# Half of an output projection taken into the attention loop, residual adds moved to GpSimd, eight output buffers

## The reference, cut to what matters

```python
xn = _layernorm(x, axis=-1)
q = _split_heads(xn @ q_w.T + q_b, 16) / sqrt(16)     # k and v the same, unscaled
attn = softmax(einsum('bhqd,bhkd->bhqk', q, k))
ctx = einsum('bhqk,bhkd->bhqd', attn, v)              # back to (1, 4096, 256)
attention = ctx @ out_w.T + out_b
acc = matmul(quant_fp8(xn), quant_fp8(weight).T)
ffn = bfloat16(acc * (x_scale * w_scale) + bias)
out = x + attention + ffn
```

## Time and profile before

| | us |
|---|---|
| three runs | 1885.83 (median), 1885.39, 1886.12 |
| the profiled execution | 1886.19 |
| its span | 1884.4 |
| ACT busy | 1764.0 (94%) |
| PE busy | 1647.7 (87%) |
| DVE busy | 1561.3 (83%) |
| POOL busy | 23.0 (1%) |

### The profile page before, as it was taken

One profiled execution on the slowest core, in us unless ns is written; L12 is line 12 of the kernel. 1 busy time (PEld: TensorE's weight loads), 2 busy tenths in 40 slices (PEclk: granted clock), 3 DMA queues, 4 the chain that ended last, 5 costly groups with the idle time before them and its releaser, 6 DMA issues.

```text
span 1884.4 us, 74586 instructions
## 1 busy us (share of the span) xinstructions
PE 1647.7 (87%) x33418; PEld 556.7 (30%) x33418; DVE 1561.3 (83%) x1924; ACT 1764.0 (94%) x1944; POOL 23.0 (1%) x41
## 2 busy tenths in 40 slices
PE   7988888888888888888888888888888888888888
PEld 4632222222222222222222222222222222222226
DVE  8687878978787888878787987878888887878788
ACT  2389999999999999999999999999999999999990
POOL 0000000000000000000000000000000000000000
PEclk9999999999999999999999999999999999999999
DMA  6430100000010000000010000001000000001003
GB/s 195 159 91 10 32 10 21 14 18 24 18 24 10 24 12 16 24 18 24 10 31 8 17 20 18 24 10 31 10 23 12 18 24 18 24 10 26 13 14 107
DMA packets 94965, 57.19 MB, mean 30 GB/s; under 512 B 55280, under 2 KB 87280, under 8 KB 94640
## 3 DMA queue, kind: packets, MB, share of 16 engines
q1 hardware_dynamic: 94160, 52.18, 10.3%
q10 hardware_dynamic: 480, 0.20, 0.0%
HBM read 30.54 MB, written 17.30 MB: 25 GB/s over the span
## 4 chain that ended last, share of the span: by engine, by line
ACT 52%; issue 33%; PE 12%; DVE 3%; ACTq 1%; DMA 0%; SPq 0%; DVEq 0%
ACT probs L667 52%; PE banks L1300 3%; PE banks L1259 3%; PE banks L1156 3%; PE banks L1388 1%; PE banks L1167 1%; ACTq L666 1%; DVE o_junk L951 1%; DVE o_sb L950 1%; PE banks L1378 0%; DVE xn_all L821 0%; DMA qk_bias<-in_L_attn_k_b_dram 0%; PE banks L1140 0%; DVE stats L736 0%; DVE x8T L834 0%
## 5 line engine op out<-in xcount | busy, mean ns | idle before, releaser
L667 ACT ACTIVATE probs<-banks 128x1024 f32<-128x1024 f32 x1888 | 1730.9, 1192 | 0.1
L1300 PE MATMUL banks<-probs,v_st 64*32 64x512 f32 x15104 | 1003.8, 590 | 2.2
L1259 PE MATMUL banks<-q_st,k_st 50*32 50x512 f16 x16384 | 792.4, 381 | 212.2 <-ACT probs L667 209.2
L1259 PEld LDWEIGHTS banks<-q_st,k_st 50*32 50x32 f16 x16384 | 232.6, 89 | 1145.5 <-ACT probs L667 1088.9
L984 DVE SCALAR_TENSOR_TENSOR horner<-horner,bits 128x1024 f32<-128x1024 f32 x320 | 393.0, 1228 | 11.0
L1300 PEld LDWEIGHTS banks<-probs,v_st 64*32 64x32 f32 x15104 | 272.0, 106 | 66.8 <-DVE o_junk L951 11.5
L971 DVE TENSOR_SCALAR bits<-banks 128x1024 int32<-128x1024 f32 x160 | 196.0, 1225 | 76.5 <-PE banks L1259 76.3
L984 DVE SCALAR_TENSOR_TENSOR horner<-bits 128x1024 f32<-128x1024 f32 x160 | 196.1, 1226 | 5.5
L989 DVE SCALAR_TENSOR_TENSOR d_probs<-horner,powers 128x1024 f32<-128x1024 f32 x160 | 196.0, 1225 | 5.5
L950 DVE COPY o_sb<-banks 128x512 f32<-128x512 f32 x32 | 22.2, 692 | 130.9 <-PE banks L1300 97.9
L980 DVE TENSOR_SCALAR bits<-bits 128x1024 int32<-128x1024 int32 x160 | 111.1, 694 | 5.5
(11 more groups left out here) (103 smaller groups left out, 428.1 us busy)
## 6 DMA issues: line engine op xcount, KB each, us to landing
k_st<-k_parts SPq DMA_DIRECT2D x102, 64.0 KB, 2.2
q_st<-q_parts SPq DMA_DIRECT2D x198, 32.0 KB, 1.9
k_st<-k_parts SPq DMA_DIRECT2D x102, 60.0 KB, 2.2
q_st<-neg_row SPq DMA_DIRECT2D x264, 1.0 KB, 1.7
xnT_copy<-probs SPq DMA_DIRECT2D x8, 512.0 KB, 3.1
q_parts<-x8T SPq DMA_DIRECT2D x16, 256.0 KB, 3.0
k_parts<-x8T SPq DMA_DIRECT2D x16, 256.0 KB, 2.4
w_f<-xnT_copy SPq DMA_DIRECT2D x16, 256.0 KB, 2.9
```

The costliest lines, as they stand in the source:

```text
L667: act.activation(probs[:, at:at + WIDE * CHUNK].rearrange("p (t c) -> p t c", t=WIDE), banks[:, bank:bank + WIDE, :], ACT.Exp, bias=EXP_SHIFT,
L1259: last = pe.matmul(banks[cols, bank + g, :], k_st[rows, keys], blocks[rows, j], start=True, stop=True, tile_position=(g * GROUP, t * VCOLS))
L1300: last = pe.matmul(banks[VCOLS * qb:VCOLS * (qb + 1), 6 + half, cols], v_st[keys, kt, :], src[keys, g * CHUNK:(g + 1) * CHUNK][:, cols], s ...
```

## The change

- A unit of the sampled pass has one more place, `OUT_AT` = 63, so 66 in all. In heads 0 to 7 PE does nothing there and DVE gives the buffer back with a semaphore increment. In heads 8 to 15 PE multiplies the finished half k = 0 of `ctxT` with its half of the output weights for two token tiles: two tiles x two row halves x four column quarters, 16 matmuls with 256 columns in f32 (32 instructions), of which eight work on different tiles of the array. The two row halves land in the two banks of the buffer. DVE adds both banks to the two rows of x in `x_all` with two adds, the second waiting for the first. 16 units times two tiles are all 32 token tiles.
- In DVE's order this stands behind the fifth block and ahead of the quantising and the take of the sums.
- Waits on the count of score places are counted without the new place (`scores_given`).
- In the output stage PE projects only the half k = 1. The add of x to the feed-forward term goes from DVE to GpSimd. DVE's L1087 waits for the group before to be added there.
- There are eight output buffers in place of two. They lie in `probs`.
- The second pass, which isn't run, loads x again.

```diff
+    OUT_AT = 63
+    OUT_BUFS = 4
-        o_out = [qt[0], qt[1]]
+        o_out = [probs[:, i * CHUNK:(i + 1) * CHUNK] for i in range(2 * OUT_BUFS)]
...
-                for p in range(PAIRS + (not full)):
+                for p in range(PAIRS + 2 * (not full)):
                     if p == MAX_AT and not full:
                         order.append(None)
+                    elif p == OUT_AT and not full:
+                        order.append(())
...
+            def outputs(again):                       # gpsimd
+                for i, g in enumerate(OUT_ORDER):
+                    n = again * GROUPS_OUT + i
+                    for b in range(2):
+                        t0 = g * CT + 2 * b
+                        pool.wait_ge(y_done, n * 2 + (b + 1 + 2))
+                        pool.wait_ge(out_ready, n * 2 + (b + 1))
+                        pool.tensor_tensor(res[b][:, :].rearrange("p (t d) -> p t d", t=2), x_all[:, t0:t0 + 2, :],
+                                           y_sb[b].rearrange("p (t d) -> p t d", t=2), ALU.add).then_inc(res_done, 1)
...
+                def output_part(h, u):                # vector
+                    n = u * c.places + OUT_AT
+                    if h < FROM_HEAD:
+                        dve.sem_inc(c.d_taken, 1)
+                        dve.wait_ge(c.d_taken, taken_at(h, u, OUT_AT))
+                        return
+                    bank, t0 = take_bank(h, n), part_tiles(h, u)
+                    rows = x_all[:, t0:t0 + 2, :].rearrange("p t d -> p (t d)")
+                    dve.wait_ge(part_done, t0 // 2 + 1)
+                    dve.tensor_tensor(rows, banks[:, bank, :], rows, ALU.add).then_inc(part_added, 1)
+                    dve.wait_ge(part_added, t0 // 2 + 1)
+                    dve.tensor_tensor(rows, banks[:, bank + 1, :], rows, ALU.add).then_inc(c.d_taken, 1)
+                    dve.wait_ge(c.d_taken, taken_at(h, u, OUT_AT))
...
+                        output_part(h, u)
                         if u:
                             quantise_part(h)
                         sums(h, u, lk + MAX_LINKS)
...
+                        dve.wait_ge(res_done, n * 2 + (b + 1))
...
-                    for b in range(2):
-                        t0 = g * CT + 2 * b
-                        dve.wait_ge(y_done, n * 2 + (b + 1 + 2))
-                        dve.tensor_tensor(res[b][:, :].rearrange("p (t d) -> p t d", t=2), x_all[:, t0:t0 + 2, :],
-                                          y_sb[b].rearrange("p (t d) -> p t d", t=2), ALU.add).then_inc(res_done, 1)
-                        dve.wait_ge(out_saved[b], n * 16 + OUT_0)
-                        dve.tensor_tensor(o_out[b][:, :], banks[:, 2 + b, :], res[b][:, :], ALU.add
+                        dve.wait_ge(out_saved[n % OUT_BUFS * 2 + b], n // OUT_BUFS * 16 + OUT_0)
+                        dve.tensor_tensor(o_out[n % OUT_BUFS * 2 + b], banks[:, 2 + b, :], res[b][:, :], ALU.add
                                           ).then_inc(out_ready, 1)
...
+                def output_part(h, n):                # tensor
+                    if h < FROM_HEAD:
+                        return
+                    u, bank, t0 = n // c.places, WIDE * ((h * c.head_places + n) % BUFS), part_tiles(h, n // c.places)
+                    buffer_free(h, n)
+                    pe.wait_ge(ctx_saved[t0 // CT % UNITS], SAVES * FROM_HEAD)
+                    for j in range(2):
+                        g, i = divmod(t0 + j, CT)
+                        t = g // UNITS * CT + i
+                        for half in range(2):
+                            rows = slice(half * GROUP, (half + 1) * GROUP)
+                            for q in range(P // VCOLS):
+                                cols = slice(q * VCOLS, (q + 1) * VCOLS)
+                                last = pe.matmul(banks[cols, bank + half, j * D:(j + 1) * D],
+                                                 ctxT[rows, 0, g % UNITS, t, cols], w_sb["o"][rows, 0, :],
+                                                 start=True, stop=True, tile_position=(half * GROUP, q * VCOLS))
+                    last.then_inc(part_done, 1)
...
-                            for k in range(KD):
+                            for k in range(KD) if again else (KD - 1,):
```

More of the change, by code:

```diff
@@ L221, in program @@
         ctx_saved = [sem(f"ctx_saved{i}") for i in range(UNITS)]
+        part_done = sem("part_done")
+        part_added = sem("part_added")
+        x_back = sem("x_back")
+        x_again = sem("x_again")
         ffn_done = sem("ffn_done")
@@ L226, in program @@
         out_ready = sem("out_ready")
-        out_saved = [sem(f"out_saved{i}") for i in range(2)]
+        out_saved = [sem(f"out_saved{i}") for i in range(2 * OUT_BUFS)]
         xq_in = sem("xq_in")
@@ L285, in __init__ @@
                 self.head_takes = UNITS * len(self.takes)
+                self.head_scores = sum(1 for _ in range(UNITS) for pair in order if pair != ())
                 self.from_half_1 = min(p for p, pair in enumerate(order) if pair and pair[0] >= KT // 2)
@@ L308, in program, with scores_given, part_tiles @@
         SAVES, CTX_0 = 16 * QB, 1
+        FROM_HEAD = HEADS // KD
+        def scores_given(c, h, n):
+            u, p = divmod(n, c.places)
+            return h * c.head_scores + (u * (c.head_scores // UNITS) + sum(1 for pair in c.order[:p] if pair != ()))
+        def part_tiles(h, u):
+            return 2 * ((h - FROM_HEAD) * UNITS + u)
         first = Pass("a", False)
@@ L384, in _ @@
                          (y_done, 2), (res_done, 2), (out_ready, 2),
-                         (out_saved[0], OUT_0), (out_saved[1], OUT_0)):
+                         *((saved, OUT_0) for saved in out_saved)):
                 sp.sem_inc(s, n)
@@ L513, in attend @@
                         load_rows(c, 1, h * 2 + 2)
[L514 removed]
+                    sp.wait_ge(c.st_done, scores_given(c, h, c.places))
                     load_q(sp, c, nxt, 0)
[L516 removed]
+                    sp.wait_ge(c.st_done, scores_given(c, h, c.places + c.first_read + 1))
                     load_k(c, nxt, 2)
@@ L553, in _ @@
                 outputs_landed(1)
+                for t in range(0, NT, 8):
+                    load_x(t, t + 8, x_back)
                 attend(second)
@@ L598, in _ @@
                 pool.wait_ge(pass2_end, 3)
+                outputs(1)
         @block.scalar
@@ L1111, in _ @@
             with dve.If(ok < P):
-                for b in range(2):
-                    dve.wait_ge(out_saved[b], OUT_0 + 16 * GROUPS_OUT)
+                for saved in out_saved:
+                    dve.wait_ge(saved, OUT_0 + 16 * (GROUPS_OUT // OUT_BUFS))
+                dve.wait_ge(x_back, 16 * (NT // 8))
+                for t in range(0, NT, 2):
+                    two = x_all[:, t:t + 2, :]
+                    dve.tensor_tensor(two, two, bo_sb[:, :, :], ALU.add).then_inc(x_again, 1)
+                dve.wait_ge(x_again, NT // 2)
                 attend(second)
@@ L1332, in sampled_heads @@
                                     maximum_scores(h, n, g)
+                            elif c.order[n % c.places] == ():
+                                output_part(h, n)
                             else:
@@ L1389, in outputs @@
                                                  ctxT[:, k, u, t, :], w_sb["o"][:, k, :],
-                                                 start=(k == 0), stop=(k == KD - 1))
+                                                 start=(k == 0 or not again), stop=(k == KD - 1))
                         last.then_inc(proj_done, 1)
```

18 lines of the change are left out of this document (10 added, 8 removed).

## The result

| | before | changed |
|---|---|---|
| median of 8 runs each, us | 1886.01 (1885.39 to 1887.58) | 1892.07 (1890.57 to 1893.7) |
| profiled execution, us | 1886.19 | 1891.66 |
| its last exponential ends | 1840.83 | 1846.47 |
| its first output term starts | 1846.50 | 1854.13 |
| first output term to last output add | 34.04 | 31.57 |

The changed kernel is slower: ratio 1.003, 95% interval 1.0021 to 1.0039. Forecast were 1890.6 us and a range of 1880 to 1897. Of the 5.47 us by which the profiled executions differ, 5.64 were lost before the last exponential and 1.99 between it and the first output term (7.66 us in place of 5.67). The output stage gave 2.47 back, 0.24 came behind the last add, and 0.07 lies outside the profiled span.

The account below looks back on a forecast made before the run. ScalarE's exponentials were taken to pace attention, and a chain of waits through PE the output stage. Stalls of 5.25 us, a 1.79 us later output stage and 2.6 us saved in it gave +4.4 us: 1890.6 us, range 1880 to 1897.

Parts of the forecast that it names:

- One sign: ScalarE idle 0.3 us once in each unit from head 8 on, just behind the unit's first places, none before.
- Stall a unit: Heads 8 to 15, unit's end: place 66's buffer returns late, scores 0.35 us late; +5.25 us in 15 units.
- ScalarE's tolerance: In attention, an exponential may start no later than 0.22 us before the one ahead of it ends.
- The part's bounds: Place 63 on PE, heads 8 to 15: 32 instructions taken as 0.87 us, lower bound 0.41, upper 1.86.
- Heads 0 to 7: Attention with place 63 empty on PE: DVE's buffer is back before place 66 wants it, cost 0.
- Way to the output stage: Last unit to first output term: quantising 2.52 us later, DVE idled 0.73, so the stage starts +1.79 us.
- Output stage: Groups of 3.78 us with DVE waiting for GpSimd; stage 31.4 us against 34.04, -2.6 us.
- P: Output stage: one GpSimd add of 128x512, taken as 1.15 us, bounds 0.68 and 1.94.
- Scores in time: Rival, attention: scores stay in time between place 62 and next unit's fourth, no stall; 1885.3 us, chance 0.22.
- Both rivals on a cheap or slow GpSimd: Output stage: P 0.75 gives 1884.2 us, chance 0.12; P 1.36 gives 1894.0 us, chance 0.14.
- The sum: Whole kernel: 5.25 + 1.79 - 2.6 = +4.4 us on the profiled 1886.19 us, 1890.6 us.
- The three terms: Attention stalls +5.25 us, later start of the output stage +1.79 us, output stage itself -2.6 us.

Follow-up runs that it names:

- e2_tail_only: Changed kernel without place 63, the whole projection in the output stage, GpSimd's residual adds and eight buffers kept: 1885.97 us, ratio 0.9988 to 1.0006.
- mended stage: Changed kernel with the output stage one group ahead on DVE, PE feeding and projecting half by half: 1886.25 us, stage 25.82 us.
- e3_residual_on_dve: Changed kernel with the residual add back on DVE in the order of before, place 63 and eight buffers kept: 1891.59 us, stage 31.43 us.

## Why the prediction was right, step by step

The mechanism and most of the signs came out as forecast. One sign did not: ScalarE shows no idle time of 0.3 us in a unit, only 0.06 us twice, since most of the loss is overlap that is missing. That the size of the stall came out so near is partly luck, as the first point says.

- *Stall a unit.* Forecast 0.35 us, measured 0.367; 5.25 and 5.5 us. The mechanism and the place were as walked: the part 0.86 us (0.87), place 66 waiting for the second add, three sums at 1.08 (1.09). Inside it two errors of mine cancel. The hand-overs PE to DVE to PE took about 0.14 us each in place of 0.06, so place 66 started 0.16 later than reckoned. And ScalarE's tolerance is wider than I read from the earlier trace rows. That row shows an exponential which started 0.22 us before the end of the one ahead and was in time; it doesn't show that a later one would be late. The late ones here last 1.02 us, not 1.14, so one may start 0.10 before the end of the one ahead. The exponential of place 65 started 0.11 before it and ended on pace. Place 65, which I had 0.12 late, was in time; place 61's stall was smaller for the same reason.
- *The part's bounds.* The upper one (1.86 us) was wrong arithmetic: the projection's 3.72 us are four token tiles and the part has two, so half of it is 1.86 with both k and 0.93 with one. The value taken was right.
- *Heads 0 to 7.* Nothing, as said.
- *Way to the output stage.* Forecast 1.79, measured 1.99. In the kernels with both adds a wait of 0.2 us appears ahead of one small instruction (L1155); with one add it is absent. What it waits for I haven't settled.
- *Output stage.* 31.4 and 31.57, group 3.78 and 3.78; the flag took 1.25 us in place of 1.1. What I said of the stage before was wrong in part: its 34.04 us hold neither the 1.29 us of the store nor 1.1 for the flag, they are PE's chain throughout (`e2_tail_only`). The sum takes the 34.04 as measured, so it didn't suffer. P was 1.11 from start to start and 1.15 long, where I took 1.15. The Trainium skill's figure in "GPSIMD Engine Reference", section 3.1, gave an estimate of 1.12 and its section 4.1 about twice DVE's time; it is 1.15 / 0.69 = 1.7 times.
- *The rivals.* Scores in time is what happens with one add, and gave the total that was named for it (1885.3, measured 1885.26), though it also has a shorter way to the stage (6.76 us, where that total had 7.46), so that agreement is partly luck. Both rivals on a cheap or slow GpSimd fell with P.
- *The sum.* +4.4 forecast, +5.5 in the profiled pair and +6.1 between the medians. The three terms make up 0.25, 0.2 and 0.13 of the difference in the profiled pair, 0.14 more came before the last exponential and 0.24 behind the last add; 0.07 lies outside the span, and what is left between profile and median is within the spread of the changed kernel's runs.

Of what the change was worth to PE, 1.7 us of its work in each of eight groups, only 2.0 us in all reached the end (33.57 to 31.57): the order on DVE left PE idle.

Not tried: the two row halves of the small form summed in one bank, which would need them ordered, and the three late sums moved apart in the planner.

## What to carry to other kernels

When one engine is saturated and the others feed it through few buffers, the price of added work is not its duration but when it gives its buffer back, and what queue of work stands right behind it. Write down for each place the latest time at which its data may arrive; the same product cost 0 us a unit with one add, 0.25 or 0.31 with one add and another tiling, 0.37 with two adds, and 0.53 with two adds at another place. Work taken off an engine in a stage shows only if the order on the others lets stages overlap: change the order together with it, and look for the loop that the new order closes.

## What the runs showed of the hardware

- An exponential of 128x1024 that comes late lasts 1.02 us; in a row that is fed in time one ends 0.917 us behind the other, although their records last up to 1.2 us and more. The 0.10 of overlap is lost when an exponential starts only at the end of the one ahead or behind it; started 0.11 us before that end it lost nothing.
- Products of different tiling next to each other overlap less, by 0.07 us against 0.18 for those of one tiling: from the sum to the scores 2.03 us (128x128) and 1.98 us (128x32) where the same arithmetic in 64x32 took 1.72.
- GpSimd's add lasted 1.15 us and DVE's instructions 0.69 and 0.74 us when they ran side by side in the mended stage; DVE's took 0.68 and 0.74 without GpSimd (`e3_residual_on_dve`).
- TensorE's granted clock fell in the output stage, where PE is less busy now than before. Busy time by stretch of the changed kernel (PE, weight loads, DVE, ScalarE, GpSimd, then the granted clock, DMA share, GB/s):

```profile
1846.00:1854.00 8.00, 4.72 (x56) 2.59 (x40) 7.27 (x16) 0.47 (x1) 0.00 (x0) 1.00 0.25 74
1854.00:1858.00 4.00, 2.36 (x11) 1.48 (x12) 2.90 (x6) 0.00 (x0) 2.27 (x2) 0.75 0.21 39
1858.00:1862.00 4.00, 4.00 (x14) 2.87 (x13) 2.92 (x6) 0.00 (x0) 2.26 (x2) 0.50 0.45 160
1862.00:1866.00 4.00, 4.00 (x24) 3.43 (x22) 3.00 (x5) 0.00 (x0) 2.27 (x2) 0.90 0.42 149
```

  0.50 is the level of 1.2 GHz. PE had waited 2.83 us for DVE just ahead of it; in the kernel before its longest wait there was 1.19 us, and the clock stayed at 1.00. In the changed kernel it cost next to nothing, because PE wasn't the bound: one of DVE's terms started 0.17 us late, and its group took 3.80 us in place of 3.78. In the mended stage the clock was 0.64 from 1858 to 1862 us, a feed of four took 1.04 us in place of 0.61 and the projection behind it 1.91 in place of 1.03, and the second group's output add waited 1.58 us for PE.
